# All of y, and B, turned by VectorE in the paired groups, with x units 2 and 3 kept ahead of y of chunks 2 and 3

## The chip, the core and the metric

One core of a Trainium2 chip runs the whole program; the metric is its device time in microseconds (us), median of three runs. Engines: TensorE (PE; PEld is its weight load), VectorE (DVE), ScalarE (ACT), GpSimd (POOL), SyncE (SP, it starts most DMAs). Each works through its own queue in order and waits on semaphores for the others.

## The reference, cut to what matters

```
x   = layernorm(hidden)                       # 2048 tokens x 1024
gate, xBC, dt = x @ in_proj                   # gate and x 4096 wide, B and C 8 groups x 128
xBC = silu(causal_conv4(xBC))                 # 4 taps along the tokens
y   = scan over tokens, 64 heads of 64, state 128   # state = state*exp(dt*A) + dt*x*B ; y = state*C + D*x
yn  = y * rsqrt(mean(y*y over the 512 of a group) + eps) * norm_weight * silu(gate)
out = hidden + yn @ out_proj + ffn(x)         # ffn: 1024x1024 and a rank-16 LoRA, 2 of 8 experts
```
Everything is float32 and must come out as such.

## The kernel before, in words

The 2048 tokens are four blocks q of 512 (TB), a block is four chunks c of 128 (Q). The 4096 channels are eight groups g of 512 (8 heads). A group's stages on TensorE are: four gate units (gate of the group, 128 channels each), four slots of output projection of the group before (`out_units`, two halves each), six units of x, B and C of the group after (`x_unit` 0 to 5; 4 is B and 5 is C), and among them the chunked scan of the group itself. A unit is 8 k-tiles of 128x128 weights with three matmuls each of 512 columns, since float32 is made of a high and a low part (`three`, lines L1072 to L1074: hi*hi, hi*lo, lo*hi). Three PSUM banks (pX, dense1, dense0) are used in turn, so TensorE may run three units ahead of whoever empties them.

The scan of a chunk: C B^T goes into pCB (`chunk_1`, L1163), is masked with the decays E (`masked`, DVE), and multiplies dt*x into pY or pD0 (`chunk_2y`, L1187); the state read gives pS (`chunk_2s`), the state update pU (`chunk_2b`). `y_state`, `y_skip` and `y_intra` sum y on DVE; ACT squares and scales it (`mean_square`, `normalize`, with GpSimd's power in `inv_rms`), giving yn with tokens on partitions. It must be turned to channels on partitions, multiplied by the gate and split in high and low for the projection.

Block 0 uses `group`, where PE turns x, B and y. Blocks 1 to 3 use `group` for g = 0 and `paired_group` for g = 1 to 7. There x is turned by DVE in 32x32 blocks (`x_rows`: for two chunks 16 instructions of 32 partitions x 256), B too (`B_rows`: for all four chunks 16 instructions of 32x128), and y of chunks 0 and 1 (`yn_rows`, 16 of 32x256, L1658), then `gated_pair`, `z_high_pair` (ACT) and `gated_lo_pair` on 1024 columns. y of chunks 2 and 3 is turned by PE: `chunk_3` is four transposes of 128x128 into pD0 (L1217), in the next group behind its gate units 0 and 2 (in group 7 between its last units), and DVE and ACT finish them chunk by chunk with `gated` (L1640), `z_high`, `gated_lo` (L1647).

The order on every engine is written out by hand in `paired_group`; nothing is planned at run time. Chains that tie DVE and ACT: `conv_taps(j)` on DVE (three dependent instructions, L1497) needs `ev_conv(j)` on ACT, that needs `silu(j-2)` on DVE and stands behind `tanh_conv(j-1)`, which needs `conv_taps(j-1)`. What TensorE takes from DVE early in a group: `wx` (L1555), which ACT splits (`wx_high`) and GpSimd (`wx_low`, L514) for `chunk_2b(g, 0)`; `B_lo`; and z_lo of chunk 3 for the first `out_units`.

Of the kernel before, what the change touches and what calls it, by code (L numbers as in the profile page):

```python
# [83 lines left out]
def layer_kernel(nc, x_tok, x_tr, w_slots, group_const, dt_bias, a_log, d_skip, b_base, lora_b, out_tr):  # L84
    ctx = ExitStack()
    with ctx:
# [17 lines left out]
        xT = [sb(f"xT{i}", [128, XT, TB]) for i in range(2)]  # L104
        BC = [sb(f"BC{i}", [128, 2, TB]) for i in range(2)]
# [56 lines left out]
        x_tm = sb("x_tm", [128, 2, GC])  # L162
        B_tm = sb("B_tm", [128, NC, N])
# [89 lines left out]
        bt_done = sem("bt_done")  # L253
# [59 lines left out]
        def bt_n(q, g):  # L313
            return (q - 1) * (G - 1) + g
# [304 lines left out]
        def _(act):  # L619
# [39 lines left out]
            def block_body(q, first_block, last_block):  # L659
# [60 lines left out]

                def wx_high(g, c):
                    act.wait_ge(xw_done, chunk(q, g, c) * 2 + 2)
                    nc.scalar.activation(wx_hi[:], wx[:], ACT.Copy).then_inc(wx_hi_done, 1)  # L723

                def chunk_1(g, p, c, last=False, behind_exp=None, two=False, behind_wx=None):
                    n, E_c = chunk(q, g, c), E_2[half_of(two, c)]
                    E_flat = E_c.rearrange("p h t -> p (h t)")
                    act.wait_ge(s1, n * 2 + 2)
                    if two:
                        act.wait_ge(bt_done, bt_n(q, g))  # L730
                    nc.scalar.activation(B_hi[:], B_tm[:, c, :] if two else pCB[:, 0:N], ACT.Copy).then_inc(ck_evac, 1)
                    if not (first_block and c == 0):
                        nc.scalar.activation(C_hi[:], CT[p][:, c * Q:(c + 1) * Q], ACT.Copy)
                    if not (first_block and c == 0):
                        act.wait_ge(s_upd, grp(q, g) * S_STEPS + (c + 2 if c else 1))
                        nc.scalar.activation(S_hi[:], state_at(g, c), ACT.Copy).then_inc(cs_hi, 1)  # L736


                    if behind_wx is not None:
                        wx_high(g, c)  # L740
                        behind_wx()
# [12 lines left out]
                    if behind_exp is not None:  # L754
                        behind_exp()
                    if behind_wx is None and not (last_block and c == NC - 1):
                        wx_high(g, c)
                    if c >= 1 and not two:
                        normalize(g, c - 1)

                    if c < 2:
                        load_cum(g, c + 2)
                    elif not last:
                        load_cum(g + 1, c - 2)

# [25 lines left out]
                def z_high_pair(g, p):  # L791
                    act.wait_ge(z_done, chunk(q, g, 0) * 2 + (2 + 4))
                    nc.scalar.activation(z_hi[:, :, 0:2 * Q], xT[p][:, :, 0:2 * Q], ACT.Copy).then_inc(zhi_done, 2)
# [152 lines left out]
                def paired_group(g, p, second=True, last=False):  # L946
# [9 lines left out]
                    normalize(g - 1, 3, second)  # L956
                    gate_unit(1)
                    chunk_1(g, p, 0, last, two=True)
                    z_high(g - 1, 3)
                    skip(g, 0)  # L960
                    gate_unit(2)
                    gate_unit(3)
                    skip(g, 1)
                    chunk_1(g, p, 1, last, two=True)
# [4 lines left out]
                    def normalize_pair():  # L969
                        normalize(g, 0, True)  # L970
                        normalize(g, 1, True)

                    chunk_1(g, p, 2, last, two=True, behind_wx=normalize_pair)
# [5 lines left out]
                    chunk_1(g, p, 3, last, two=True)  # L979
                    skip(g, 3)  # L980
                    z_high_pair(g, p)
# [5 lines left out]
                    mean_square(g, 3, True)  # L987
                    if last:
                        normalize(7, 2, True)
                        normalize(7, 3, True)  # L990
                        z_high(7, 2)
                        z_high(7, 3)
                    else:
                        normalize(g, 2, True)
                        x_unit(5)
                        z_high(g, 2)
                        tanh_conv(g, 5)
# [38 lines left out]
        def _(pe):  # L1036
# [22 lines left out]
            def block_body(q, first_block, last_block):  # L1059
# [114 lines left out]
                def chunk_2y(g, c, two=False):  # L1174
# [3 lines left out]
                    if r == 0:  # L1178
                        pe.wait_ge(y_done, n + 1)
                    else:  # L1180
                        pe.wait_ge(*((y_done, n) if c == NC - 1 else (z_done, n * 2 + (1 + 4 - 4))))
                    pe.wait_ge(xw_done, n * 2 + 1)
# [24 lines left out]
                def chunk_3(g, c, after_router=False, two=False):  # L1207
# [5 lines left out]
                    if two:  # L1213
                        pe.wait_ge(y_done, n - c % 2 + (2 + 1))
# [3 lines left out]
                    mm.then_inc(s3, 3 if two and c == 2 else 1)  # L1218
# [108 lines left out]
                def paired_group(g, p, second=True, last=False):  # L1327
# [8 lines left out]
                    if second:  # L1336
                        chunk_3(g - 1, 2, two=True)
                    gate_unit(g, False, 1, True)
                    chunk_1(g, 0, p, True, True)
                    gate_unit(g, False, 2, True)  # L1340
                    chunk_3(g - 1, 3, two=second)
# [61 lines left out]
        def _(dve):  # L1403
# [61 lines left out]
            def block_body(q, first_block, last_block):  # L1465
# [21 lines left out]
                def conv_taps(g, j, p):  # L1487

                    r, n = j % 2, (post_n(q, g + 1, j) - 1) * 3

                    if j == 0:
                        dve.wait_ge(consts_ready, q * PREPS + (1 if g is NO_GROUP else g + 2))
                    dve.wait_ge(evac_act, act_n(q, g, 4 + j))
                    for t in range(3):
                        if t:
                            dve.wait_ge(taps, n + t)
                        nc.vector.scalar_tensor_tensor(out=conv_u[r], in0=conv_in[r][:, t:t + TB],  # L1497
                                                       scalar=const_g[p][:, 4 * j + t:4 * j + t + 1], in1=conv_u[r],
                                                       op0=ALU.mult, op1=ALU.add).then_inc(taps, 1)
# [15 lines left out]
                def x_rows(g, c, p, first, end):  # L1515

                    if first == 0:
                        dve.wait_ge(post, post_n(q, g, XT - 1))
                        dve.wait_ge(xd_done, chunk(q, g, c) + 1)
                        dve.wait_ge(xw_done, chunk(q, g, c) * 2)  # L1520
                    for f in range(first, end):
# [7 lines left out]
                def B_rows(g, p, first, end):  # L1529

                    if first == 0:
                        dve.wait_ge(post, post_n(q, g, XT))
                        dve.wait_ge(ck_evac, chunk(q, g, 0))
                        dve.wait_ge(bl_done, chunk(q, g, 0))
                    for f in range(first, end):
                        for k in range(4):
                            src = BT[p][32 * f:32 * f + 32, :].rearrange("n (c t) -> n c t", c=NC)[:, :, 32 * k:32 * k + 32]
                            ins = nc.vector.transpose(B_tm[32 * k:32 * k + 32, :, 32 * f:32 * f + 32], src)
                    if end == 4:
                        ins.then_inc(bt_done, 1)  # L1540

                def chunk_1_x(g, c, two=False):
# [4 lines left out]
                    x_c = x_tm[:, c % 2, :] if two else pX[:]  # L1547
                    if two:
                        dve.wait_ge(xt_done, xt_n(q, g, c))
                    else:  # L1550
                        dve.wait_ge(s1, n * 2 + 1)
                    nc.vector.tensor_tensor(heads(dtx_2[half_of(two, c)]), heads(x_c), per_head(0, c), ALU.mult)\
                        .then_inc(xw_done, 1 if updates else 2)
                    if updates:
                        nc.vector.tensor_tensor(heads(wx[:]), heads(x_c), per_head(1, c), ALU.mult).then_inc(xw_done, 1)  # L1555

                def chunk_1_cb(g, c, two=False):
# [3 lines left out]
                    nc.vector.tensor_tensor(B_lo[:], B_tm[:, c, :] if two else pCB[:, 0:N], B_hi[:].bitcast(F32), ALU.subtract)\  # L1561
                        .then_inc(bl_done, 1)
# [71 lines left out]
                def gated(g, c):  # L1634
# [3 lines left out]
                    dve.wait_ge(s3, n + 1)  # L1638
# [543 lines left out]
```

## Time and profile before

| | |
|---|---|
| median of 3 runs | 3144.74 us (3143.58 to 3145.55) |
| profiled execution | 3145.09 us, its span 3143.4 us |
| PE busy | 3126.1 us, 99% of the span |
| DVE busy | 2558.5 us, 81% |
| ACT busy | 1704.5 us, 54% |
| POOL busy | 835.5 us, 27% |
| granted TensorE clock | 1.000 |

The span goes from the first to the last instruction of one profiled execution; the run's time is 1.7 us longer. A start and a duration stand in each row of a timeline; matmuls overlap one another, so their cost is the distance from start to start. The square bracket behind a row is the idle time of that engine just before it, and who ended it.

### The profile page before, as it was taken

How to read it: one execution, taken by the hardware profiler on the slowest of the kernel's cores; microseconds unless marked ns; L12 is line 12 of the kernel's file. 1: busy time of each engine (PE TensorE's matmuls, PEld its weight loads, DVE VectorE, ACT ScalarE, POOL GpSimd, SP SyncE). 2: the span in 40 equal slices, each digit the busy share in tenths (PEclk: the TensorE clock that was granted, in tenths of full speed). 3: DMA queues.
4: the chain of work that ended last, by engine and by line, in shares of the span. 5: the costliest groups of instructions: out<-in, count | busy, mean ns of one | idle time of the engine just before them, and what ended most of it. 6: DMA issues, size and time to landing. Idle time of an engine off the chain costs nothing.

```text
span 3143.4 us, 55218 instructions
## 1 busy us (share of the span) xinstructions
PE 3126.1 (99%) x17660; PEld 2573.4 (82%) x17660; DVE 2558.5 (81%) x4599; ACT 1704.5 (54%) x4467; POOL 835.5 (27%) x917
## 2 busy tenths in 40 slices
PE   8999999999999999999999999999999999999999
PEld 7788888887888888888788888888878888888887
DVE  7977777785589999999648999999954988989983
ACT  5766666664265555656226555556533655565551
POOL 4444434433022222222103222222210222222220
PEclk9999999999999999999999999999999999999999
DMA  8777777777665555555566555555546555555554
GB/s 290 274 265 272 264 276 266 261 256 263 232 216 194 189 201 187 189 194 201 173 225 205 191 191 191 201 184 190 209 166 236 196 195 187 195 194 201 186 189 161
DMA packets 185668, 672.63 MB, mean 214 GB/s; under 512 B 21056, under 2 KB 22208, under 8 KB 185408
## 3 DMA queue, kind: packets, MB, share of 16 engines
q1 hardware_dynamic: 161280, 584.91, 53.3%
q10 hardware_dynamic: 24128, 84.42, 7.6%
q8 instruction: 142, 2.33, 0.3%
q14 instruction: 118, 0.97, 0.1%
HBM read 532.41 MB, written 136.84 MB: 213 GB/s over the span
## 4 chain that ended last, share of the span: by engine, by line
PE 95%; DVE 2%; ACT 1%; DMA 1%; issue 0%; SPq 0%; POOL 0%; ACTq 0%; DVEq 0%; POOLq 0%
PE dense L1072 21%; PE dense L1074 21%; PE dense L1073 21%; PE pX L1072 7%; PE pX L1074 7%; PE pX L1073 6%; PE pY L1187 3%; PE pD L1217 1%; PE pD L1187 1%; DVE conv_us L1497 1%; PE pCB L1163 1%; PE pU L1072 1%; PE pS L1073 1%; PE pS L1072 1%; PE pS L1074 1%; PE pU L1074 1%
## 5 line engine op out<-in xcount | busy, mean ns | idle before, releaser
L1072 PE MATMUL dense<-xn_hi,w_hl 128*128 128x512 f32 (+2 forms) x2192 | 869.7, 397 | 0.8 <-POOL w_hl L444 0.5
L1074 PE MATMUL dense<-xn_hi,w_hl 128*128 128x512 f32 (+2 forms) x2192 | 853.7, 389 | 0.0
L1073 PE MATMUL dense<-xn_lo,w_hl 128*128 128x512 f32 (+2 forms) x2192 | 852.0, 389 | 0.0
L1497 DVE SCALAR_TENSOR_TENSOR conv_us<-conv_in,const_g,conv_us 128x512 f32<-128x512 f32 x576 | 480.3, 834 | 47.0 <-ACT conv_us L694 33.2
L1074 PEld LDWEIGHTS dense<-xn_hi,w_hl 128*128 128x128 f32 (+1 forms) x2192 | 409.5, 187 | 88.9
L1072 PEld LDWEIGHTS dense<-xn_hi,w_hl 128*128 128x128 f32 (+1 forms) x2192 | 409.9, 187 | 86.0 <-issue 2.2
L1073 PEld LDWEIGHTS dense<-xn_lo,w_hl 128*128 128x128 f32 (+1 forms) x2192 | 410.3, 187 | 83.5 <-issue 1.2
L1072 PE MATMUL dense<-z_hi,w_hl 128*128 128x512 f32 x820 | 324.4, 396 | 1.6 <-DVE acc L1680 1.1
L501 POOL TENSOR_TENSOR C_lo<-BC,C_hi 128x128 fp32r<-128x128 f32 x120 | 60.0, 500 | 983.5 <-ACT S_hi L736 982.9
L1074 PE MATMUL dense<-z_hi,w_hl 128*128 128x512 f32 x820 | 319.7, 390 | 0.0
L1073 PE MATMUL dense<-z_lo,w_hl 128*128 128x512 f32 x820 | 319.1, 389 | 0.0
L1525 DVE STREAM_TRANSPOSE x_tm<-xT 32x256 f32<-32x256 f32 x672 | 292.8, 436 | 11.8
L1072 PE MATMUL pX<-xn_hi,w_hl 128*128 128x512 f32 x696 | 274.4, 394 | 0.0
L625 ACT ACTIVATE w_hl<-w_raw 128x512 fp32r<-128x512 f32 x244 | 148.0, 628 | 229.2 <-PE dense L1074 123.4
L1074 PE MATMUL pX<-xn_hi,w_hl 128*128 128x512 f32 x696 | 271.2, 390 | 0.0
L1073 PE MATMUL pX<-xn_lo,w_hl 128*128 128x512 f32 x696 | 270.7, 389 | 0.0
L444 POOL TENSOR_TENSOR w_hl<-w_raw,w_hl 128x512 fp32r<-128x512 f32 x122 | 166.6, 1367 | 285.1 <-ACT w_hl L625 285.0
L521 POOL TENSOR_TENSOR rstd<-ssq,eps_t 128x1 f32<-128x1 f32 x128 | 41.6, 325 | 713.6 <-ACT yn L779 515.4
L1680 DVE TENSOR_TENSOR acc<-acc,dense 128x512 f32<-128x512 f32 x205 | 140.3, 685 | 95.5 <-PE dense L1074 86.5
L700 ACT ACTIVATE conv_in<-conv_us 128x512 f32<-128x512 f32 x192 | 120.9, 630 | 175.5 <-DVE conv_us L1497 171.7
L514 POOL TENSOR_TENSOR wx_lo<-wx,wx_hi 128x512 fp32r<-128x512 f32 x120 | 160.1, 1334 | 188.1 <-ACT wx_hi L723 188.1
L746 ACT ACTIVATE E<-cum_b,tok_g 128x128 f32<-128x128 f32 x688 | 210.0, 392 | 0.0
(233 smaller groups left out, 5935.3 us busy)
## 6 DMA issues: line engine op xcount, KB each, us to landing
w_hl<-w_split SPq DMA_DIRECT2D x732, 512.0 KB, 3.5
w_split<-w_hl SPq DMA_DIRECT2D x244, 512.0 KB, 3.8
cum_b<-cum_scratch ACTq DMA_DIRECT2D x128, 512.0 KB, 4.9
w_raw<-w_slots_dram SPq DMA_DIRECT2D x122, 512.0 KB, 5.4
acc<-x_tr_dram ACTq DMA_DIRECT2D x16, 512.0 KB, 6.5
out_tr_dram<-acc ACTq DMA_DIRECT2D x16, 512.0 KB, 4.7
BC<-x_tok_dram SPq DMA_DIRECT2D x6, 512.0 KB, 5.3
conv_us<-x_tok_dram SPq DMA_DIRECT2D x6, 512.0 KB, 6.2
```

The costliest lines, as they stand in the source:

```text
L444: nc.gpsimd.tensor_tensor(w_hl[s][:, 0, 1, :], w_raw[s][:, 0:512], w_hl[s][:, 0, 0, :].bitcast(F32), ALU.subtract).then_inc(lo0_done, 1)
L514: nc.gpsimd.tensor_tensor(wx_lo[:], wx[:], wx_hi[:].bitcast(F32), ALU.subtract).then_inc(wx_lo_done, 1)
L625: nc.scalar.activation(w_hl[s][:, h, 0, :], w_raw[s][:, 512 * h:512 * h + 512], ACT.Copy).then_inc(hi_done, 1)
L700: nc.scalar.activation(conv_in[j % 2][:, 0:TB], conv_u[j % 2], ACT.Tanh).then_inc(tanh_done, 1)
L746: ins = nc.scalar.activation(E_c[:, h, :], cum_b[c % 2][:, h, :], ACT.Relu, scale=-1.0, bias=tok_g[:, 4 * NC + c, h:h + 1])
L1072: nc.tensor.matmul(out, lhs[0], rhs[0], start=start, stop=False)
L1073: nc.tensor.matmul(out, lhs[0], rhs[1], start=False, stop=False)
L1074: return nc.tensor.matmul(out, lhs[1], rhs[0], start=False, stop=stop)
L1187: mm = nc.tensor.matmul(pY_c[t, h * P:(h + 1) * P], E_c[:, h, t], dtx_c[:, h * P:(h + 1) * P], start=True, stop=True)
L1497: nc.vector.scalar_tensor_tensor(out=conv_u[r], in0=conv_in[r][:, t:t + TB], scalar=const_g[p][:, 4 * j + t:4 * j + t + 1], in1=conv_u[r], ...
L1525: ins = nc.vector.transpose(dst[:, :, :, 32 * f:32 * f + 32], src[:, :, c:c + 2, 32 * k:32 * k + 32])
L1680: nc.vector.tensor_tensor(acc[:, i, :], acc[:, i, :], b[:], ALU.add).then_inc(evac_dve, 1)
```

## The change

On DVE and ACT of the paired groups:
- `x_tm` becomes [128, 2, 640] and xT and BC one tensor `xBC`, so that `x_rows` turns x and B of two chunks with one set of 16 instructions of 32x320; `B_rows` and its semaphore go.
- `yn_rows`, `gated_pair`, `z_high_pair` and `gated_lo_pair` take a chunk and are used for chunks 2 and 3 as well; `chunk_3`, `gated`, `z_high` and `gated_lo` stay for group 0's chunk 3 alone.
- DVE's order at the end of a group is: x units 2 and 3, then y of chunk 3 (`y_state` to `y_intra`), taps of unit 4, and the turning of y in four parts with the three taps of unit 5 one by one between them; silu of unit 5 and `prep` move into the next group's `x_rows`. `chunk_1_x` and `chunk_1_cb` are taken apart (`wx_product`, `dtx_product`, `b_low`, `cb_masked`).
- ACT normalizes both chunks 2 and 3 before x unit 5; its `chunk_1` is taken apart in `b_high`, `cs_high`, `ramps`, `next_cum`.

On PE: `chunk_3` of chunks 2 and 3 goes, `chunk_1(g, 0)` stands behind gate unit 2 instead of 1, `chunk_1(g, 1)` behind `out_units(g, 1)` instead of before it.

The diff's core (PE, then DVE; ACT's order follows the same moves):

```diff
                     gate_unit(g, False, 0, True)
-                    if second:
-                        chunk_3(g - 1, 2, two=True)
                     gate_unit(g, False, 1, True)
+                    gate_unit(g, False, 2, True)
+                    if not second:
+                        chunk_3(0, 3)
                     chunk_1(g, 0, p, True, True)
-                    gate_unit(g, False, 2, True)
-                    chunk_3(g - 1, 3, two=second)
                     gate_unit(g, False, 3, True)
...
                     out_units(g, 0, two=True)
+                    out_units(g, 1, two=True)
                     chunk_1(g, 1, p, True, True)
-                    out_units(g, 1, two=True)
...
-                    x_units(2)
-                    if last:
-                        chunk_3(7, 2, two=True)
-                        x_units(1)
-                        chunk_3(7, 3, two=True)
-                        x_units(1)
+                    x_units(4 if last else 2)
```

```diff
-                            src = xT[p][32 * f:32 * f + 32, :, :].rearrange("n j (c t) -> n j c t", c=NC)
-                            dst = x_tm[32 * k:32 * k + 32, :, :].rearrange("p c (j i) -> p j c i", j=XT)
+                            src = xBC[p][32 * f:32 * f + 32, 0:XT + 1, :].rearrange("n j (c t) -> n j c t", c=NC)
+                            dst = x_tm[32 * k:32 * k + 32, :, :].rearrange("p c (j i) -> p j c i", j=XT + 1)
...
-                    x_rows(g, 0, p, 1 if second else 0, 4)
-                    chunk_1_x(g, 0, True)
-                    gated(g - 1, 3)
-                    chunk_1_cb(g, 0, True)
-                    gated_lo(g - 1, 3)
+                    x_rows(g, 0, p, 0, 1)
+                    if second:
+                        silu(g - 1, 5, p)
+                        prep(g)
+                    x_rows(g, 0, p, 1, 4)
+                    wx_product(g, 0)
+                    if second:
+                        gated_lo_pair(g - 1, 1 - p, 2)
+                        b_low(g, 0)
+                    else:
+                        gated(0, 3)
+                        b_low(g, 0)
+                        gated_lo(0, 3)
                     gate_tile(g, 0, False)
                     gate_tile(g, 1, False)
-                    masked(g, 0, True)
+                    cb_masked(g, 0)
+                    dtx_product(g, 0)
+                    y_state(g, 0, True)
+                    y_skip(g, 0, True)
+                    state(g, 0)
                     gate_tile(g, 2, False)
+                    gate_tile(g, 3, False)
...
+                    wx_product(g, 1)
+                    dtx_product(g, 1)
+                    b_low(g, 1)
                     out_adds(g, 0, halves=(0,), two=True)
+                    masked(g, 0, True)
+                    out_adds(g, 0, halves=(1,), two=True)
                     x_rows(g, 2, p, 0, 1)
...
                     else:
-                        silu(g, 5, 1 - p)
-                        B_rows(g + 1, 1 - p, 2, 4)
-                        prep(g + 1)
+                        x_unit(2)
+                        x_unit(3)
+                        y_state(g, 3, True)
+                        y_skip(g, 3, True)
+                        state(g, 3)
+                        y_intra(g, 2, True)
+                        y_intra(g, 3, True)
+                        conv_taps(g, 4, p)
+                        silu(g, 3, 1 - p)
+                        yn_rows(g, p, 2, 0, 1)
+                        conv_tap(g, 5, p, 0)
+                        yn_rows(g, p, 2, 1, 2)
+                        conv_tap(g, 5, p, 1)
+                        yn_rows(g, p, 2, 2, 3)
+                        conv_tap(g, 5, p, 2)
+                        silu(g, 4, 1 - p)
+                        yn_rows(g, p, 2, 3, 4)
+                        gated_pair(g, p, 2)
```

## Rows read from the trace of the kernel before

**Rows 1.** The page: busy time, share of the span and instructions of an engine
```profile
PE 3126.1 (99%) x17660; PEld 2573.4 (82%) x17660; DVE 2558.5 (81%) x4599; ACT 1704.5 (54%) x4467; POOL 835.5 (27%) x917
```

**Rows 2.** TensorE's waits: who for, us in total, times, longest
```profile
PE pCB L1052 <- ACT xT L638: 8.6, 1, 8.6
```

**Rows 3.** TensorE's timeline in one paired group: start, duration, engine, line, operation
```profile
1103.82 0.39 PE L1072 MATMUL pX<-xn_hi,w_hl 128*128 128x512 f32 x1
...
1109.26 0.60 PE L1217 MATMUL pD<-ident,yn 128*128 128x128 f32 x4
...
1115.19 0.38 PE L1163 MATMUL pCB<-BC 128*128 128x128 f32 x2
...
1120.91 0.60 PE L1217 MATMUL pD<-ident,yn 128*128 128x128 f32 x4
...
1126.81 0.39 PE L1072 MATMUL pS<-S_hi,C_hi 128*128 128x512 f32 x1
...
1127.49 0.39 PE L1072 MATMUL pU<-wx_hi,B_hi 128*128 128x512 f32 x1
```

**Rows 4.** Windows in blocks 1 and 3: busy us of PE, PEld, DVE, ACT, POOL; clock; DMA
```profile
1115.80:1203.90 88.10, 88.10 (x506) 73.01 (x505) 80.96 (x152) 50.86 (x142) 22.05 (x24) 1.00 0.55 192
...
2667.20:2754.60 87.40, 87.40 (x503) 72.43 (x502) 78.64 (x150) 50.44 (x140) 19.36 (x22) 1.00 0.56 193
```

**Rows 5.** VectorE's groups by line and form: busy, mean ns, idle before
```profile
L1525 DVE STREAM_TRANSPOSE x_tm<-xT 32x256 f32<-32x256 f32 x672 | 292.8, 436 | 11.8
...
L1538 DVE STREAM_TRANSPOSE B_tm<-BC 32x128 f32<-32x128 f32 x336 | 101.7, 303 | 5.2
```

**Rows 6.** VectorE's timeline from one group's unit 4 to the next one's
```profile
1101.64 2.32 DVE L1497 SCALAR_TENSOR_TENSOR conv_us<-conv_in,const_g,conv_us 128x512 f32<-128x512 f32 x3
...
1113.37 0.69 DVE L1647 TENSOR_TENSOR z_lo<-z_t,z_hi 128x512 fp32r<-128x512 f32 x1 [0.70 <-ACT z_hi L789]
...
1114.70 2.52 DVE L1538 STREAM_TRANSPOSE B_tm<-BC 32x128 f32<-32x128 f32 x8
...
1123.79 0.69 DVE L1555 TENSOR_TENSOR wx<-x_tm,tok_g 128x512 f32<-128x512 f32 x1
...
1124.39 0.69 DVE L1640 TENSOR_TENSOR z_t<-pD,gate 128x512 f32<-128x512 f32 x1
...
1125.78 1.40 DVE L1647 TENSOR_TENSOR z_lo<-z_t,z_hi 128x512 fp32r<-128x512 f32 x1 [0.30 <-ACT z_hi L789]
...
1133.89 0.68 DVE L1680 TENSOR_TENSOR acc<-acc,dense 128x512 f32<-128x512 f32 x1
...
1139.69 0.80 DVE L1561 TENSOR_TENSOR B_lo<-B_tm,B_hi 128x128 fp32r<-128x128 f32 x1
...
1149.06 0.68 DVE L1611 TENSOR_TENSOR y<-y,pY 128x512 f32<-128x512 f32 x1
...
1153.82 1.78 DVE L1658 STREAM_TRANSPOSE xT<-yn 32x256 f32<-32x256 f32 x4 [1.27 <-ACT yn L785]
...
1156.33 5.40 DVE L1658 STREAM_TRANSPOSE xT<-yn 32x256 f32<-32x256 f32 x12
...
1164.95 1.22 DVE L1666 TENSOR_TENSOR xT<-xT,gate 128x1024 f32<-128x1024 f32 x1
...
1189.72 2.32 DVE L1497 SCALAR_TENSOR_TENSOR conv_us<-conv_in,const_g,conv_us 128x512 f32<-128x512 f32 x3
```

**Rows 7.** VectorE's timeline in block 3, B_lo of chunk 1
```profile
2603.78 1.29 DVE L1561 TENSOR_TENSOR B_lo<-B_tm,B_hi 128x128 fp32r<-128x128 f32 x1
```

**Rows 8.** ScalarE's and GpSimd's timelines behind unit 4 and behind wx
```profile
1104.25 0.62 ACT L700 ACTIVATE conv_in<-conv_us 128x512 f32<-128x512 f32 x1
...
1105.39 0.78 ACT L694 ACTIVATE conv_us<-dense,const_g 128x512 f32<-128x512 f32 x1
...
1104.09 0.88 POOL L523 TENSOR_TENSOR rstd<-rstd,eps_t 128x1 f32<-128x1 f32 x1
...
1125.22 1.40 POOL L514 TENSOR_TENSOR wx_lo<-wx,wx_hi 128x512 fp32r<-128x512 f32 x1 [3.96 <-ACT wx_hi L723]
```

More of the change, by code:

```diff
@@ L723, in wx_high, with ramps @@
                     nc.scalar.activation(wx_hi[:], wx[:], ACT.Copy).then_inc(wx_hi_done, 1)
-                def chunk_1(g, p, c, last=False, behind_exp=None, two=False, behind_wx=None):
+                def ramps(g, c, two=False):
                     n, E_c = chunk(q, g, c), E_2[half_of(two, c)]
                     E_flat = E_c.rearrange("p h t -> p (h t)")
[L728 to L741, printed above, removed]
@@ L753, in chunk_1, with next_cum @@
                                              scale=-1.0).then_inc(exp_done, 1)
[L754 to L759, printed above, removed]
+                def next_cum(g, c, last):
                     if c < 2:
@@ L764, in chunk_1 @@
                         load_cum(g + 1, c - 2)
+                def chunk_1(g, p, c, last=False, behind_exp=None):
+                    b_high(g, c)
+                    cs_high(g, p, c)
+                    ramps(g, c)
+                    if behind_exp is not None:
+                        behind_exp()
+                    wx_high(g, c)
+                    if c >= 1:
+                        normalize(g, c - 1)
+                    next_cum(g, c, last)
                 def skip(g, c):
@@ L955, in paired_group @@
                     gate_unit(0)
-                    normalize(g - 1, 3, second)
+                    if second:
+                        z_high_pair(g - 1, 1 - p, 2)
+                    else:
+                        normalize(0, 3)
+                    cs_high(g, p, 0)
                     gate_unit(1)
-                    chunk_1(g, p, 0, last, two=True)
-                    z_high(g - 1, 3)
+                    b_high(g, 0, True)
+                    wx_high(g, 0)
+                    if not second:
+                        z_high(0, 3)
                     skip(g, 0)
@@ L962, in paired_group @@
                     gate_unit(3)
+                    b_high(g, 1, True)
+                    ramps(g, 0, True)
+                    next_cum(g, 0, last)
                     skip(g, 1)
-                    chunk_1(g, p, 1, last, two=True)
+                    wx_high(g, 1)
+                    cs_high(g, p, 1)
+                    ramps(g, 1, True)
+                    next_cum(g, 1, last)
                     if last:
@@ L968, in paired_group @@
                     mean_square(g, 1, True)
[L969 to L973, printed above, removed]
+                    b_high(g, 2, True)
+                    cs_high(g, p, 2)
+                    wx_high(g, 2)
+                    normalize(g, 0, True)
+                    normalize(g, 1, True)
+                    ramps(g, 2, True)
+                    next_cum(g, 2, last)
                     skip(g, 2)
@@ L978, in paired_group @@
                         tanh_conv(g, 0)
-                    chunk_1(g, p, 3, last, two=True)
+                    b_high(g, 3, True)
+                    cs_high(g, p, 3)
+                    wx_high(g, 3)
+                    ramps(g, 3, True)
+                    next_cum(g, 3, last)
                     skip(g, 3)
-                    z_high_pair(g, p)
+                    z_high_pair(g, p, 0)
                     if not last:
@@ L1217, in chunk_3 @@
                         mm = nc.tensor.transpose(pD0[:, j * 128:(j + 1) * 128], yn[c % 2][:, j * 128:(j + 1) * 128], ident[:])
-                    mm.then_inc(s3, 3 if two and c == 2 else 1)
+                    mm.then_inc(s3, 1)
                 def dt_slot(first_tile, end_tile):
@@ L1527, in x_rows, with wx_product, dtx_product, b_low @@
                         ins.then_inc(xt_done, 1)
[L1529 to L1542, printed above, removed]
+                def wx_product(g, c):
+                    if last_block and c == NC - 1:
+                        return
+                    if c == 0:
+                        dve.wait_ge(prep_done, q * PREPS + g + 2)
+                    dve.wait_ge(xt_done, xt_n(q, g, c))
+                    nc.vector.tensor_tensor(heads(wx[:]), heads(x_tm[:, c % 2, 0:GC]), per_head(1, c), ALU.mult).then_inc(xw_done, 1)
+                def dtx_product(g, c):
+                    dve.wait_ge(xt_done, xt_n(q, g, c))
+                    nc.vector.tensor_tensor(heads(dtx_2[c % 2]), heads(x_tm[:, c % 2, 0:GC]), per_head(0, c), ALU.mult)\
+                        .then_inc(xw_done, 2 if last_block and c == NC - 1 else 1)
+                def b_low(g, c):
+                    dve.wait_ge(ck_evac, chunk(q, g, c) + 1)
+                    nc.vector.tensor_tensor(B_lo[:], x_tm[:, c % 2, GC:GC + N], B_hi[:].bitcast(F32), ALU.subtract)\
+                        .then_inc(bl_done, 1)
+                def cb_masked(g, c):
+                    dve.wait_ge(s1, chunk(q, g, c) * 2 + 2)
+                    nc.vector.tensor_tensor(CBm, pCB[:, N:N + Q], causal[:], ALU.mult).then_inc(cbm_done, 1)
+                def chunk_1_x(g, c):
                     n = chunk(q, g, c)
@@ L1648, in gated_lo, with yn_rows @@
                         .then_inc(z_done, 1)
-                def yn_rows(g, p, first, end):
+                def yn_rows(g, p, c, first, end):
                     if first == 0:
-                        dve.wait_ge(yn_done, chunk(q, g, 1) + 1 + 1)
+                        dve.wait_ge(yn_done, chunk(q, g, c) + 2 + 1)
                     for f in range(first, end):
@@ L1963, in group @@
                             silu(g, 5, 1 - p)
-                        if not first_block:
-                            B_rows(g + 1, 1 - p, 0, 4)
                         prep(g + 1)
@@ L2061, in paired_group @@
                             ln_stats(q + 1, 2)
[L2062 to L2063 removed]
+                        gated_lo_pair(7, 1, 2)
                         if not last_block:
@@ L2067, in paired_group @@
                     else:
-                        silu(g, 5, 1 - p)
-                        B_rows(g + 1, 1 - p, 2, 4)
-                        prep(g + 1)
+                        x_unit(2)
+                        x_unit(3)
+                        y_state(g, 3, True)
+                        y_skip(g, 3, True)
+                        state(g, 3)
+                        y_intra(g, 2, True)
+                        y_intra(g, 3, True)
+                        conv_taps(g, 4, p)
[9 more added lines that the diff above has]
+                        gated_pair(g, p, 2)
                 group(0, 0, first=True)
```

200 lines of the change are left out of this document (105 added, 95 removed).

## The prediction

> **What bounds the kernel now.** I read the page first: PE is busy for 3126.1 of 3143.4 us, DVE for 2558.5, 81% [rows 1]. So TensorE's sum of work is the time, and every transpose taken from it is worth its full price, if nobody becomes slower than TensorE. Its waits say the same: the longest is 8.6 us, once, at the end of a block, and in the paired groups there is none [rows 2]. Next I laid DVE's timeline beside TensorE's over two groups. A paired group lasts 88.08 us: unit 4's taps begin at 1101.64 and again at 1189.72 [rows 6], and all units of DVE, ACT and PE repeat with that distance. The window shows TensorE busy through all of it and DVE for 80.96 of 88.10 [rows 4].
>
> The 7.1 idle us are not to be had. In DVE's timeline the brackets name ACT, never TensorE (0.70, 0.30, 1.27 are shown) [rows 6]: DVE hands something to ACT and takes it back. DVE and ACT thus form a loop of their own. How much longer than that loop TensorE's 88.08 is, one row tells: `B_lo` of chunk 1 at 1139.69 takes 0.80 instead of 0.28, since it ends when GpSimd ends its `wx_lo`, and that hangs on ACT, which waited for TensorE's C B^T. In block 3, where the state of the last chunk is not updated, TensorE's group is 0.7 us shorter [rows 4] and DVE has 1.2 less to do, and the same row takes 1.29 [rows 7]: 0.5 more, as it must if this is the slack. So the slack of DVE's loop is 0.52 us a group in blocks 1 and 2 and 1.01 in block 3. **The kernel has two bounds, 0.5 us in 88 apart.**
>
> **What the change takes from TensorE.** A unit of 24 matmuls takes 1109.26 - 1103.82 = 5.44 us. With the four transposes in front the next takes 5.93, the other one 5.90 (1126.81 - 1120.91) [rows 3]. So a `chunk_3` costs 0.47 us, and 14 of them in 3 blocks are 42 x 0.47 = 19.9 us. TensorE's group becomes 87.13. The moved `chunk_1` costs the same in its new place (5.72 - 5.44 = 0.28). If that were all: 3145.1 - 19.9 = 3125.
>
> **What it gives to DVE, a group at a time.**
> - 16 more turns of y: 12 take 5.40 [rows 6], 0.45 each, 7.19 in all.
> - `B_rows` goes: 16 turns, 2.52 for 8 [rows 6], -5.04.
> - `x_rows` has 32 turns of 320 elements a partition, which the trace lacks. Below: 436 ns, as with 256; above: 436 + 303, as if B were turned on its own [rows 5]. Between 128 and 256 an element costs (436 - 303)/128 = 1.04 ns, so 320 take about 503; I take this: 32 x 0.067 = +2.1 (ends 0 and, by halves of B's 16 turns, +5).
> - gate and low part for two chunks at once, 1.22 for 1024 columns against twice 0.60 from start to start (1123.79 to 1124.39) [rows 6]: -0.1.
> - Work: 7.2 - 5.0 + 2.1 - 0.1 = +4.2 us, against 0.5 of slack and 0.95 that TensorE gives up.
>
> **The new order, followed from unit 4's taps (E = 0).** Before, the first `out_adds` began at 1133.89, E + 32.25 [rows 6]. Now: taps(4) and silu(3) to 2.9. The turning of chunks 2 and 3 needs both normalized; GpSimd's last power ends at 1104.09 + 0.88 = E + 3.3 [rows 8], the scaling on ACT 0.7 later: 4.15, DVE idles 1.25. Tanh(4) and `ev_conv(5)` stand behind it on ACT and last 1.92 (1104.25 to 1105.39 + 0.78) [rows 8]: the first tap of unit 5 at 6.1. Four parts of y (7.2), three single taps (2.0) and silu(4) end at 14.2; `gated_pair` 15.4; first part of x 17.5; silu(5), `prep` 18.6; the rest of x 24.8: `wx`. Then `gated_lo_pair` to 26.6, `b_low` 27.9 (it meets GpSimd's `wx_lo` as z_lo did, 1.40 instead of 0.69 [rows 6]), two gate tiles 29.1, mask and dt*x 29.9, `y_state`, `y_skip`, `state` 31.9, two gate tiles 33.1, `wx`, dt*x, `B_lo` of chunk 1: 34.5. That is 2.25 later, and `masked(g, 0)`, 1.2, is still to come. To `y_intra(g, 0)` it was 15.17 (1133.89 to 1149.06); now + 1.2 (mask), + 1.1 (x), + 0.2 (`y_skip` right behind `y_state`), - 0.8 (`B_lo` is done): 16.7. From there to the next E nothing changes but the place of waits: 40.66. **Loop: 34.5 + 16.7 + 40.7 = 91.9 us**, above TensorE's 87.1. In block 3 it was 1.2 shorter without slack (86.4 against 87.6): 90.7 now, 87.4 before.
>
> SBUF — State Buffer of the Trainium skill ("Who interferes with whom") says that of a GpSimd instruction and a VectorE one with two SBUF inputs the first to start holds the shared ports to its end. The two rows of `B_lo` and z_lo agree. By it `wx_lo` would wait for `gated_lo_pair` and `B_lo` end at 28.3: 0.4 more a group, 6 us in all; it is in the upper end only.
>
> **Where TensorE pays.** It needs `wx_lo`, 2.83 us after `wx` began (1123.79 to 1125.22 + 1.40) [rows 6, 8]: E + 27.6. It stands at `chunk_2b(g, 0)` at 1127.49 = E + 25.85 [rows 3], 0.95 earlier without transposes: 24.9. So in group 2 it stalls 2.7 us, net + 1.8. From there to group 7 it goes with the loop, five times: 5 x 3.8 = 19.0 in blocks 1 and 2, 5 x 3.3 = 16.5 in block 3. Group 7 has nine units in place of six and 9 adds in place of taps, and is bound by TensorE again (- 0.95 for its transposes). Sum: 3 x 1.8 + 2 x 19.0 + 16.5 - 3 x 0.95 = 57.0. Against the profiled execution's 3145.1: 3202.1; the median of the runs lies 0.35 below it: **3202 us**.
>
> The Trainium skill (VectorE: DVE Perf Modes, "Rules for kernel authors") says to turn 128x128 on TensorE if the result may lie in PSUM, which speaks against the change. Its figures, however (311 ns on VectorE for 128x128 in bf16), would make eight tiles 2.5 us instead of 7.19 and the loop 87.2, an estimate from that page: the time would be about 3127. The float32 rows decide, 3.6 us a chunk on DVE against 0.47 on TensorE.
>
> **Rivals.**
> - *TensorE stays the bound, 3125 us.* For it: PE 99%, DVE 81% on the page, and z no longer waits for PSUM and two trips to ACT. Against: it needs a loop under 87.1, thus nearly 5 us less than I laid out, while only 1.9 of the old waits (0.8, 0.4 and 0.7 around z_lo) leave. The place is the start of a group: from `wx` at E + 22 on TensorE stalls; faster than before it is with a loop under about 88. Chance 0.11.
> - *The waits fall together.* DVE's new wait for the normalized chunks (1.25) and GpSimd's lock (0.9) are hidden, or 320 elements cost as 256: a loop of 89.7 and 88.5. No stall in group 2, 2 x 5 x 1.6 + 5 x 1.1 - 3 x 1.9 = + 16: 3161. Chance 0.15, with all between.
> - *Longer still.* Lock, single taps that drain one by one, and masks that wait for ACT's `skip(g, 1)`, which now ends 0.6 before its buffer is needed: 93 to 93.5, 15 x 1.3 more: 3222. Chance 0.08.
> - *It cancels:* a loop of just 88, 3145. Chance 0.04.
>
> **Chances.** The forecast, 3185 to 3220, has 0.62. This measurement tells 0.2% (6 us) from no change: faster 0.11, same 0.04, slower 0.85. The range from 3155 to 3222 leaves out the two cases near and below 3145, and a little above.
>
> **What would show it.** PE's busy share falls from 99% to about 97%, with waits in `paired_group` that were not there: some 3 us at L1072 pU for GpSimd's wx_lo in every group from 2 on, about 1 at pY or pD for the second mask. The distance of unit 4's taps is 91.9 in blocks 1 and 2 and 90.7 in block 3. The new turns of x have a mean of 500 ns. DVE is busy for over 85 us of a group, with a bracket of 1.2 for yn before the second `yn_rows`. Wrong it is if that distance is TensorE's 87.1 with PE at 99%, or if TensorE waits for the projection's banks instead.

## The result, and the profile after

The changed kernel takes 3224.9 us (median of 4 runs, 3223.1 to 3225.6) against 3144.2 for the kernel before: ratio 1.0255, 95% interval 1.0238 to 1.0273. It is 80.8 us slower. Forecast were 57: the direction and the place of the stall are right, the size is not.

The page of the changed kernel, engines' busy time and the chain that ended last:

```profile
PE 3146.2 (98%) x17492; PEld 2577.6 (80%) x17492; DVE 2651.1 (82%) x4557; ACT 1706.1 (53%) x4446; POOL 847.8 (26%) x917
...
PE 44%; DVE 29%; issue 14%; ACT 7%; POOL 3%; DMA 1%; DVEq 0%; ACTq 0%; SPq 0%; POOLq 0%
```

and that chain of the kernel before:

```profile
PE 95%; DVE 2%; ACT 1%; DMA 1%; issue 0%; SPq 0%; POOL 0%; ACTq 0%; DVEq 0%; POOLq 0%
```

Against [rows 1] TensorE has 168 instructions fewer (42 `chunk_3` of four) and yet is busy for 20 us more. VectorE has only 93 us more work in 3224. Its 82% would not tell anybody that it is the bound; the chain does, with more than half of it outside TensorE where it was 5%.

TensorE's waits, which were 8.6 us once [rows 2]:

```profile
PE pU L1107 <- DVE B_lo L1576: 55.8, 18, 3.2
PE pCB L1087 <- ACT xBC L645: 8.7, 1, 8.7
PE pCB L1198 <- issue: 3.1, 11, 0.5
PE pD L1222 <- DVE w_raw L1618: 2.1, 2, 1.1
```

Eighteen waits of 3.1 us: groups 2 to 7 of three blocks, all ahead of chunk 0's state update. That is where the forecast put them.

VectorE's timeline over one group of block 1 (start, duration, engine, line, operation; idle before in brackets), which answers to [rows 6]:

```profile
1200.48 2.32 DVE L1523 SCALAR_TENSOR_TENSOR conv_us<-conv_in,const_g,conv_us 128x512 f32<-128x512 f32 x3
...
1204.60 1.77 DVE L1694 STREAM_TRANSPOSE xBC<-yn 32x256 f32<-32x256 f32 x4 [1.20 <-ACT yn L804]
1206.43 0.75 DVE L1523 SCALAR_TENSOR_TENSOR conv_us<-conv_in,const_g,conv_us 128x512 f32<-128x512 f32 x1
...
1225.44 0.69 DVE L1567 TENSOR_TENSOR wx<-x_tm,tok_g 128x512 f32<-128x512 f32 x1
1226.05 1.22 DVE L1707 TENSOR_TENSOR z_lo<-xBC,z_hi 128x1024 fp32r<-128x1024 f32 x1
1227.18 1.35 DVE L1576 TENSOR_TENSOR B_lo<-x_tm,B_hi 128x128 fp32r<-128x128 f32 x1
...
1235.06 0.68 DVE L1717 TENSOR_TENSOR acc<-acc,dense 128x512 f32<-128x512 f32 x1
...
1239.51 0.52 DVE L1732 TENSOR_SCALAR const_g<-consts 128x34 f32<-128x34 f32 x1
...
1252.43 0.68 DVE L1647 TENSOR_TENSOR y<-y,pY 128x512 f32<-128x512 f32 x1
...
1293.02 0.74 DVE L1523 SCALAR_TENSOR_TENSOR conv_us<-conv_in,const_g,conv_us 128x512 f32<-128x512 f32 x1
```

`B_lo` (1227.18) and `const_g` (1239.51) take longer than the 0.28 and 0.18 us that they take elsewhere: each starts inside one of GpSimd's instructions and ends with it, to 0.15 us:

```profile
1226.87 1.51 POOL L521 TENSOR_TENSOR wx_lo<-wx,wx_hi 128x512 fp32r<-128x512 f32 x1 [4.23 <-ACT wx_hi L750]
...
1238.69 1.29 POOL L508 TENSOR_TENSOR S_lo<-S_cur,S_hi 128x512 fp32r<-128x512 f32 x1
```

The loop is 1293.02 - 1200.48 = 92.54 us. One loop of block 3 has 2803.43 - 2711.88 = 91.55:

```profile
2711.88 1.53 DVE L1523 SCALAR_TENSOR_TENSOR conv_us<-conv_in,const_g,conv_us 128x512 f32<-128x512 f32 x2
...
2803.43 0.74 DVE L1523 SCALAR_TENSOR_TENSOR conv_us<-conv_in,const_g,conv_us 128x512 f32<-128x512 f32 x1
```

The turns of x with B, and VectorE's busy time in one loop (columns of the window as in [rows 4]), against 80.96 of 88.10 before:

```profile
L1557 DVE STREAM_TRANSPOSE x_tm<-xBC 32x320 f32<-32x320 f32 x672 | 337.6, 502 | 10.0
```

```profile
1146.98:1239.51 92.53, 89.25 (x498) 73.16 (x497) 85.46 (x149) 50.97 (x142) 22.52 (x25) 0.98 0.56 182
```

TensorE's timeline at the wait, which answers to the last of [rows 3]:

```profile
1228.59 0.50 PE L1107 MATMUL pU<-wx_hi,B_hi 128*128 128x512 f32 x1 [3.06 <-DVE B_lo L1576]
...
1229.78 0.63 PE L1108 MATMUL dense<-z_lo,w_hl 128*128 128x512 f32 x1
1230.21 0.63 PE L1109 MATMUL dense<-z_hi,w_hl 128*128 128x512 f32 x1
...
1233.05 0.40 PE L1107 MATMUL dense<-z_hi,w_hl 128*128 128x512 f32 x1
```

From 1229.8 on the matmuls start 0.43 us apart (1230.21 - 1229.78) instead of 0.23: behind the wait TensorE runs at 1.2 GHz for some 3 us. Granted clock of 4.4 us windows behind the wait, one in a loop of block 1, then behind the last wait (group 7) of each block (span, PE busy, clock, DMA share, GB/s):

```profile
1228.60:1233.00 4.40, 4.40 (x12) 0.61 0.02 4
1506.20:1510.60 4.40, 4.40 (x13) 0.64 0.00 0
2309.03:2313.43 4.40, 4.40 (x10) 0.50 0.00 0
3107.68:3112.08 4.40, 4.40 (x10) 0.50 0.00 0
```

The clock falls in this way behind 16 of the 18 waits; behind two, in block 3, it does not (18.1 us to the next state update, as against 19.4 to 21.0 in the other loops and 17.95 before). y_turns_cut below has the same TensorE instructions at a granted clock of 1.000 and is busy for 3113.7 us, so the slow clock makes TensorE busier by 3146.2 - 3113.7 = 32.5 us. That was not in the forecast. How much of it reaches the time is another question, which the experiments take up.

### The profile page after: what moved, and what is told of

It is laid out like the page before. It is cut to its first block, busy times and chain, and to the rows that moved or that the text cites. A ratio compares the mean times of both kernels' runs of the same rounds, so it can differ in the third digit from the quotient of the medians.

```text
span 3223.9 us, 54734 instructions
## 1 busy us (share of the span) xinstructions
PE 3146.2 (98%) x17492; PEld 2577.6 (80%) x17492; DVE 2651.1 (82%) x4557; ACT 1706.1 (53%) x4446; POOL 847.8 (26%) x917
## 4 chain that ended last, share of the span: by engine, by line
PE 44%; DVE 29%; issue 14%; ACT 7%; POOL 3%; DMA 1%; DVEq 0%; ACTq 0%; SPq 0%; POOLq 0%
PE dense L1107 11%; PE dense L1109 11%; PE dense L1108 11%; DVE x_tm L1557 8%; DVE xBC L1694 6%; DVE conv_us L1523 4%; DVE acc L1717 2%; PE pY L1222 2%; PE pX L1109 1%; PE pX L1107 1%; PE pX L1108 1%; DVE E L1618 1%; DVE xBC L1535 1%; DVE B_lo L1576 1%; ACT w_raw L790 1%
## 5 line engine op out<-in xcount | busy, mean ns | idle before, releaser
L1108 PEld LDWEIGHTS dense<-xn_lo,w_hl 128*128 128x128 f32 (+1 forms) x2192 | 410.1, 187 | 85.8 <-issue 2.6
L1557 DVE STREAM_TRANSPOSE x_tm<-xBC 32x320 f32<-32x320 f32 x672 | 337.6, 502 | 10.0
L1107 PE MATMUL dense<-z_hi,w_hl 128*128 128x512 f32 x820 | 337.1, 411 | 2.0 <-DVE acc L1717 1.5
L1694 DVE STREAM_TRANSPOSE xBC<-yn 32x256 f32<-32x256 f32 x672 | 293.1, 436 | 53.0 <-ACT yn L804 42.9
L508 POOL TENSOR_TENSOR C_lo<-xBC,C_hi 128x128 fp32r<-128x128 f32 x120 | 60.2, 501 | 1031.2 <-ACT S_hi L744 1030.5
L1108 PE MATMUL dense<-z_lo,w_hl 128*128 128x512 f32 x820 | 328.9, 401 | 0.0
L1109 PE MATMUL dense<-z_hi,w_hl 128*128 128x512 f32 x820 | 328.2, 400 | 0.0
L528 POOL TENSOR_TENSOR rstd<-ssq,eps_t 128x1 f32<-128x1 f32 x128 | 53.3, 416 | 737.8 <-ACT yn L798 540.6
```

The source lines that it names most:

```text
L1107: nc.tensor.matmul(out, lhs[0], rhs[0], start=start, stop=False)
L1108: nc.tensor.matmul(out, lhs[0], rhs[1], start=False, stop=False)
L1109: return nc.tensor.matmul(out, lhs[1], rhs[0], start=False, stop=stop)
L1694: ins = nc.vector.transpose(dst[:, :, :, 32 * k:32 * k + 32], src[:, :, :, 32 * f:32 * f + 32])
```

## The experiments

The two theories after the first look: **A**, VectorE's loop with ScalarE sets the period, and its length is the sum of VectorE's work; the slow clock behind each wait lies inside the next wait and costs nothing, but for the last of a block. **B**, a good part of the 80.8 us is something else: the slow clock, or the new order itself. Two expectations name narrower ones: **C**, only the chain of hand-offs from unit 4 to chunk 0's state update counts; **D**, B in x's squares and its new waits are the cause.

**y_turns_cut.** The changed kernel with 12 of 16 turns of y of chunks 2 and 3 left out in the loops (that part of y stays unturned).

```
-                        for k in range(4):
+                        for k in range(1 if c == 2 else 4):      # yn_rows
```

> The changed kernel with 12 of the 16 turns of y of chunks 2 and 3 left out (those squares of y keep old values): 5.4 us less of VectorE's work a group, at the place between unit 4's taps and wx. Theory A (VectorE and ScalarE are one loop that is too long, 92.5 us against TensorE's 87.1): the loop falls to 87.1, the wait before pU of chunk 0 goes, about 3126 us. Theory B (what costs is TensorE's clock, which falls behind each wait): also about 3126, since the wait goes with it. This run shows only that the turns of y are the price; if it stays above 3160, both are wrong and the order on ScalarE or TensorE is the cause.

Measured: 3143.3 us, ratio 0.9993 (0.9984 to 1.0003): the whole loss is gone, but nothing beyond it, where 3126 was expected. The period is 88.5. Two rows of VectorE say why, behind unit 4:

```profile
1284.95 0.43 DVE L1694 STREAM_TRANSPOSE xBC<-yn 32x256 f32<-32x256 f32 x1 [1.20 <-ACT yn L804]
1286.78 0.75 DVE L1523 SCALAR_TENSOR_TENSOR conv_us<-conv_in,const_g,conv_us 128x512 f32<-128x512 f32 x1 [1.39 <-ACT conv_us L701]
```

The first tap of unit 5 cannot start before ScalarE has scaled y of chunk 3, done tanh(4) and copied unit 5 out. With four turns ahead of it the turns hid that; with one, 1.39 us of wait appear. 92.54 - 12 x 0.448 (5.38) + 1.39 = 88.55. So VectorE's loop stays the bound even here, just above TensorE's 87.1, and cutting 5.4 us of its work returned 4.0. TensorE's own wait moved with it, from chunk 0's state update to the second masked product, which waits for VectorE once in each loop:

```profile
PE pD L1222 <- DVE w_raw L1618: 12.0, 15, 1.1
```

What follows: VectorE's loop sets the period, as A says, but A's plain sum of work missed: the loop has a floor that is ScalarE's.

**x_turns_cut.** The same cut in `x_rows` for chunks 2 and 3 (12 turns of 320 elements, 6.0 us; part of x and B is left unturned).

> The changed kernel with 12 of the 16 turns of x and B of chunks 2 and 3 left out (those squares keep the values of chunks 0 and 1): 6.2 us less of VectorE's work a group, but in the middle of it, not on the way from unit 4's taps to wx. Theory A in its plain form (only the sum of VectorE's loop counts): loop 86.4, TensorE is the bound, 3125. Theory C (only the way from unit 4 to pU of chunk 0 counts, 28.0 us from the taps to B_lo): nothing changes, 3225. Between them, theory A with a second loop through TensorE (unit 4's end, its evacuation 1.7, the way of 28.0, TensorE's 59.0 from pU to unit 4's end: 88.7): a wait of 1.5 us stays, 3157, or 3190 if each wait costs 2.1 us of slow clock as well.

Measured: 3184.0 us, ratio 1.0117 (1.0101 to 1.0134), between A's plain 3125 and C's 3225, and inside the 3157 to 3190 of a second loop through TensorE. First TensorE's waits, all at the old place; then VectorE's in four loops of block 1:

```profile
PE pU L1107 <- DVE B_lo L1576: 40.6, 18, 2.4
```

```profile
DVE acc L1717 <- PE pX L1109: 8.9, 6, 1.5
DVE pCB L1581 <- PE pCB L1198: 6.4, 4, 1.6
...
DVE acc L1717 <- PE dense L1109: 1.8, 4, 0.5
```

In the changed kernel the same stretch has no wait of VectorE for TensorE. Here there are 17.1 us of them, 4.3 a loop: the loop now runs through TensorE, which is itself late by its wait at the group's start. TensorE's state updates of chunk 0 lie 89.82, 91.45, 89.79 and 91.44 us apart. The windows from an update to the next, in the same order, tell the two lengths apart (columns as above):

```profile
1040.88:1058.98 18.10, 18.09 (x81) 1.00 0.59 199
1130.70:1150.42 19.72, 19.72 (x80) 0.91 0.57 185
1222.15:1240.23 18.08, 18.08 (x80) 1.00 0.60 201
1311.94:1331.64 19.70, 19.70 (x80) 0.91 0.55 188
```

Where the clock falls behind the wait, the loop is 1.6 us longer. So this kernel has a loop through VectorE, ScalarE and TensorE of 89.8 us, and the slow matmuls are part of it. Behind these shorter waits (1.9 to 2.4 us) the clock falls in 8 of 18 cases.

In the changed kernel the slow stretch is hidden by less. The first 24 projection matmuls behind the update must be through before VectorE's second add. In the loop shown above they are at 1236.26 + 0.39 = 1236.65, and the add starts at 1236.86:

```profile
1236.26 0.39 PE L1109 MATMUL dense<-z_hi,w_hl 128*128 128x512 f32 x1
```

```profile
1236.86 0.68 DVE L1717 TENSOR_TENSOR acc<-acc,dense 128x512 f32<-128x512 f32 x1
```

So there are 0.2 us to spare. In two of the 15 loops the stretch was 1.3 us longer (21.0 us to the next update), these adds moved back by 1.2 and 1.1 us, and the loop took 93.67 for 92.53 and 92.96 for 91.55.

**fill_wait.** Twenty matmuls that nobody reads (twelve in group 2) stand in front of the wait at `chunk_2b(g, 0)`, so that TensorE does not fall idle.

```
                 def chunk_2b(g, c, after_router=False, fill=0):
...
+                    if fill:
+                        pe.wait_ge(s_upd, grp(q, g) * S_STEPS + 1)
+                        for _ in range(fill):
+                            nc.tensor.matmul(pU[:], C_hi[:], S_hi[:], start=True, stop=True)
```

> The changed kernel with 20 (group 2: 12) extra matmuls of 128x512 on TensorE right before its wait for pU of chunk 0, into pU, overwritten by the true ones: 4.5 us that keep TensorE at work where it waited. Theory A: in groups 2 to 6 the slow clock only fills time that TensorE would have waited, so nothing is won there; only behind the last such wait of a block, in group 7, where TensorE is the bound again, 2.1 us come back: 3225 - 3 x 2.1 = 3219. Theory B (the clock is the cost, 2.1 us at each of 18 waits): 3225 - 38 = 3187.

Measured: 3218.4 us, ratio 1.0231 (1.0214 to 1.0248). The granted clock of the whole is 1.0 instead of 0.989, and yet only 6.5 us return: A's 3219, not B's 3187. In groups 2 to 6 the slow stretch is hidden; behind the last wait of a block nothing absorbs it.

The 6.5 are a rough price. The two kernels were timed in different sessions; against the kernel before, each in its own, the difference is 7.8. And the filling has a price of its own. Twenty matmuls take 4.5 us where the wait was 3.1:

```profile
1222.85 4.70 PE L1238 MATMUL pU<-S_hi,C_hi 128*128 128x512 f32 x20
1227.39 0.39 PE L1107 MATMUL pU<-wx_hi,B_hi 128*128 128x512 f32 x1
```

```profile
1224.66 1.38 DVE L1580 TENSOR_TENSOR B_lo<-x_tm,B_hi 128x128 fp32r<-128x128 f32 x1
```

`B_lo` is done at 1226.04 and the update starts 1.3 us behind it. It stays that late from group 3 to the end of the block, so each block pays 1.3 us once. The changed kernel's trace puts the clock at 7.1 us behind the last waits and 2.5 in the two lengthened loops. So an estimate from the run and the trace together is that 6 to 10 of the 80.8 us are the clock's.

**b_in_x_only.** The kernel before with B in x's squares: `B_rows` gone, `x_tm` 640 wide, y as before. Of the order only what this needs is moved: the first turns of x stand behind unit 5, and `B_lo` of chunk 1 ahead of the adds.

```
-                    act.wait_ge(s1, n * 2 + 2)
                     if two:
-                        act.wait_ge(bt_done, bt_n(q, g))
...
+                        act.wait_ge(xt_done, xt_n(q, g, c))
```

> The kernel before with one part of the change alone: B turned within x's squares (32 turns of 32x320 for 32 of 32x256 and 16 of 32x128), y of chunks 2 and 3 still turned by TensorE. VectorE has about 3 us less a group. Theory A: TensorE stays the bound with 88.08 a group, 3144, no change within 0.2%, and VectorE's brackets grow by 3 us. Theory D (this part and its new waits are what made the changed kernel slow): slower than 3150.

Measured: 3163.6 us, ratio 1.0057 (1.004 to 1.0073): 18 us slower than before, though VectorE's busy time fell from 2558.5 to 2512.7. ScalarE's timeline at a group's start:

```profile
1301.93 0.31 ACT L732 ACTIVATE B_hi<-x_tm 128x128 fp32r<-128x128 f32 x1 [4.71 <-DVE x_tm L1528]
...
1302.86 2.44 ACT L747 ACTIVATE E<-cum_b,tok_g 128x128 f32<-128x128 f32 x8
...
1306.25 0.62 ACT L722 ACTIVATE wx_hi<-wx 128x512 fp32r<-128x512 f32 x1
1306.77 0.62 ACT L790 ACTIVATE z_hi<-z_t 128x512 fp32r<-128x512 f32 x1
```

and VectorE's:

```profile
1302.54 0.69 DVE L1554 TENSOR_TENSOR wx<-x_tm,tok_g 128x512 f32<-128x512 f32 x1
...
1307.42 1.35 DVE L1650 TENSOR_TENSOR z_lo<-z_t,z_hi 128x512 fp32r<-128x512 f32 x1 [2.45 <-ACT z_hi L790]
```

B now comes with the last square of x, so ScalarE's `B_hi` waits for it (4.71), and the operand splits, ramps and exps of `chunk_1` (4.3 us from 1301.93 to 1306.25) stand between `wx`, done at 1303.2, and its high part. z_hi and z_lo are late behind it: a wait of 2.45 us on VectorE where there was 0.30 [rows 6]. So B in x's squares alone costs time, as D has it. That it needs only the split of ScalarE's `chunk_1` that the change brings (`wx_high` ahead of `ramps`) is a reading of these rows; no run has that split alone. The next run has the whole new order; there the loss is gone, so D is not what makes the changed kernel slow.

**y_by_tensor.** The changed kernel with its order and with B in x's squares, but y of chunks 2 and 3 turned by TensorE again.

```
                     gate_unit(g, False, 0, True)
+                    if second:
+                        chunk_3(g - 1, 2, two=True)
...
-                        yn_rows(g, p, 2, 0, 1)
-                        conv_tap(g, 5, p, 0)
...
+                        conv_taps(g, 5, p)
...
-                        gated_pair(g, p, 2)
```

> The changed kernel's order of work and its B within x's squares, but y of chunks 2 and 3 of the loops' groups is turned by TensorE again, as in the kernel before. Theory A (the 16.5 turns of 436 ns, 7.2 us a group, are what makes VectorE's loop longer than TensorE's work): VectorE's loop falls from 92.5 us to about 86, under TensorE's 88.1, the wait ahead of chunk 0's state update is gone, and the time is the kernel before's, 3144 us (3138 to 3150). Theory B (the new order itself, with VectorE's unit 5 behind ScalarE's normalize of y and the hand-offs through wx, costs a good part of the 4.5 us a group): periods above 89 us and a time over 3160 us.

Measured: 3144.0 us, ratio 0.9999 (0.999 to 1.0009). All of the 80.8 us come with y of chunks 2 and 3 on VectorE. This run also takes back what surrounds the turns (the taps of unit 5 between them, both chunks normalized first, gate and low part for two chunks at once); y_turns_cut, which leaves out turns alone, says that the turns suffice. B in x's squares and the rest of the new order cost nothing together. The period is TensorE's 88.03, and VectorE now waits for TensorE, which it never did in the loops before:

```profile
1216.33 0.69 DVE L1633 TENSOR_TENSOR y<-pS,tok_g 128x512 f32<-128x512 f32 x1 [2.27 <-PE pS L1106]
```

88.03 - 2.27 = 85.8 is VectorE's loop: the slack, 0.5 us before by the forecast's reading, is 2.3 now. That is what the change's other half earns (- 5.0 + 2.1 of turns [rows 5, 6]), and it shows nothing in the time as long as TensorE is the bound.

**last_y_by_vector.** As y_by_tensor, but y of chunks 2 and 3 of the last group of a block stays on VectorE, as the change has it. The diff is against y_by_tensor.

```
-                    x_units(2)
-                    if last:
-                        chunk_3(7, 2, two=True)
-                        x_units(1)
-                        chunk_3(7, 3, two=True)
-                        x_units(1)
+                    x_units(4 if last else 2)
...
+                        yn_rows(7, 1, 2, 0, 2)
                         x_unit(5)
+                        yn_rows(7, 1, 2, 2, 4)
```

> As y_by_tensor, but y of chunks 2 and 3 of the last group of each block stays with VectorE, where after it no loop of VectorE has to be closed within the block. TensorE is spared two sets of four turns (0.47 us each) a block. If VectorE has slack there, as the theory of the loop says (group 7 issues a third fewer conv taps), the time is 3 x 0.95 = 2.85 us under that of y_by_tensor: about 3141 us, ratio to before 0.999. If group 7 is itself closed by VectorE, the time is the same as y_by_tensor's or above it.

Measured: 3141.4 us, ratio 0.9991 (0.9981 to 1.0), against 3144.0 of y_by_tensor on the same chip: - 2.5 for the 2.85 that six `chunk_3` of 0.47 are worth. The highest of its 11 times, 3142.2, lies below the lowest of y_by_tensor's 11, 3143.3. It is the fastest of all kernels run here, 2.1 us under the kernel before, which is at the edge of what this measurement can tell. The two profiled executions agree: spans of 3142.7 and 3139.8.

**consts_behind_b_low.** The changed kernel with `consts_next` moved up.

```
                     b_low(g, 1)
+                    if not last:
+                        consts_next(g, p)
...
                     x_rows(g, 2, p, 0, 1)
-                    if not last:
-                        consts_next(g, p)
```

> The changed kernel with one op moved: const_g of the next group stands behind B_lo of chunk 1 instead of behind the first x turns of chunk 2, where it took 0.52 us instead of 0.18 beside GpSimd's subtraction. If VectorE's loop alone sets the period (theory A), what it loses in one op comes out of every group: 15 x 0.34 = 5 us, time about 3220 us, ratio to before 1.024. If the period is set by the chain of hand-offs between VectorE, ScalarE and TensorE (theory C), the time stays at 3225 us.

Measured: 3214.2 us, ratio 1.0216 (1.0202 to 1.023), 10.8 us less than the changed kernel in its own session. The two were timed in different sessions, so the 10.8 are not exact to more than a few us, but the intervals of the ratios don't meet. The op takes 0.18 us in the new place, and the loop is 92.21 instead of 92.53 in blocks 1 and 2, and 91.16 instead of 91.55 in four of block 3's five:

```profile
1143.40 0.18 DVE L1732 TENSOR_SCALAR const_g<-consts 128x34 f32<-128x34 f32 x1
...
1235.60 0.17 DVE L1732 TENSOR_SCALAR const_g<-consts 128x34 f32<-128x34 f32 x1
```

That is 5 us and A's number. What the rest is, the two profiled executions tell (they differ by 9.0). Most of it is the clock. Behind the last wait of block 2 it does not fall at all, and behind the five before it neither (18.1 us to the next state update):

```profile
1505.76:1510.16 4.40, 4.40 (x12) 0.61 0.00 0
2306.99:2311.39 4.40, 4.40 (x19) 1.00 0.01 4
```

and from there to block 3's first state update it takes 2.5 us less; at the end of block 3 it is 1.1 us. Another 2.5 us are the changed kernel's two lengthened loops, which this one does not have. Against that, 2.5 us more passed here in block 0, which the edit does not touch: so much two executions differ by themselves. What decides how far the clock falls behind a wait of 3.1 us, these runs don't show.

## Why the prediction was off, by its steps

- *Two bounds, 0.5 us apart*: right in kind. y_by_tensor, with VectorE's loop 2.3 us under TensorE's work, takes the time of the kernel before, and a loop 4.5 us above it is paid in full each time. The 0.5 itself no run isolates.
- *TensorE is spared 0.47 us a `chunk_3`*: right. last_y_by_vector got 2.5 us for six, without a stall to pay for it.
- *VectorE's + 4.2 us of work*: nearly right; 32x320 turns take 502 ns (forecast 503), and it is busy for 85.46 us of a loop, 80.96 before, + 4.5.
- *The new order, followed from E*: right to a few tenths up to the adds: wait for yn 1.20 (1.25), first tap of unit 5 at E + 5.95 (6.1), `wx` at 24.96 (24.8), first add at 34.58 (34.5); the last leg 40.59 (40.66).
- **The leg from the first add to `y_intra(g, 0)` failed**: 17.37 us for 16.7. Half of it is named and tested: `const_g` now meets GpSimd's work on the state and takes 0.52 instead of 0.18 (consts_behind_b_low gives 0.33 back in each loop). Another 0.17 is a slip in the forecast's own sum: 15.17 + 1.2 + 1.1 + 0.2 - 0.8 is 16.87 by the terms as they stand there, not 16.7, which makes its loop 92.1 us and its time some 2.5 us longer. The last 0.2 stays open. So the loop is 92.53 for 91.9 in blocks 1 and 2. In block 3 it is 91.55 for 90.7, since it is 1.0 us shorter there and not 1.2. In all: 10 x 0.63 + 5 x 0.85 = 10.6 us.
- **TensorE's clock behind a wait was no term of the sum**, and is the second miss: the forecast priced each stall at its length alone. From group 7's update to the next state update TensorE took 18.45 us before and 19.97, 21.25 and 21.23 now: + 7.1 in three blocks; two loops that it lengthened, + 2.5. fill_wait, with the price of its own filling in it, gave 6.5 back.
- **Group 2's net + 1.8 was too small**; the place is right. A wait is 3.1 us in place of 2.7, and in blocks 1 and 2 TensorE loses 0.4 us more at `pCB` ahead of it. From group 1's update to group 2's it took 91.00, 91.02 and 89.75 us for 88.08, 88.08 and 87.40: + 8.2 where 5.4 were forecast. 10.6 + 7.1 + 2.5 + 2.8 = 23.0, of the 23.8 by which the forecast of 57.0 is short. The wait of about 1 us for the second mask, which was to be a sign, came only twice.
- *SBUF — State Buffer, "Who interferes with whom"* (the Trainium skill: the first to start holds the shared ports): the trace agrees in kind, as `B_lo` of 0.28 us takes 1.35 when it starts inside GpSimd's `wx_lo`, but not in full. By the page `wx_lo` would have waited for the end of VectorE's z_lo at 1227.27. Its row starts at 1226.87 and lasts 1.51 us where it lasted 1.40 before, and `B_lo` ends at E + 28.05, between the 27.9 without that wait and the 28.3 with it. What the overlap with GpSimd did cost lay at another row, `const_g`.
- *The rivals*: "longer still", 3222, was the nearest in time (chance 0.08), but by luck more than by its mechanism. Overlap with GpSimd is in both, yet the loop is 92.5 and not 93 to 93.5; the slow clock and group 2, which that rival does not name, bring the time up to it. Nothing fell together. "TensorE stays the bound" needed a VectorE loop under 87.1; it is 5.4 us over.

## What to carry to other kernels

When two engines' loops are within a per cent of each other, work moved from one to the other costs its full price on the receiving side; take it off the loop where it has slack (here the last group of a block, where 2.5 us were to be had) and leave it where it has none. Count for a cut only what the next hand-off lets through: 5.4 us of VectorE's work returned 4.0 a loop, and 6.0 us elsewhere returned 1.9 (block 1), since there a loop through TensorE took over. Add to every new wait of TensorE of some 3 us the slow matmuls behind it (1.5 to 2.8 us here, in most cases), where nothing downstream absorbs them.

## What the hardware showed beyond that

- After waits of the same 3.1 us the granted clock was 0.50, 0.50 and 0.64 over 4.4 us in one kernel's blocks, and 0.61 and 1.00 in another's; behind waits of 1.9 to 2.4 us it fell in 8 of 18 cases. A change worth 5 us by its mechanism measured as 10.8, with this as the main part of the rest.
- Twenty matmuls (4.5 us) in the place of a 3.1 us wait held the clock at 1.0 and cost 1.3 us a block, once, for being longer than the wait. The same slow stretch cost 1.6 us a loop in x_turns_cut and nothing in most loops of the changed kernel, by which loop was the longer.
- An op of 128x34 elements can cost three times its time by where it stands: 0.18 us, or 0.52 when it starts inside GpSimd's `S_lo`.
